# Propagation steps of a GNN kernel: nine kept blocks and a ring of four slots of two

## The reference

```python
wn = w * inv_sqrt_out[s] * inv_sqrt_in[d]
def step(h, _):
    agg = jax.ops.segment_sum(h[s] * wn[:, None], d, num_segments=n)
    return ((1.0 - ALPHA) * agg + ALPHA * feat_0, None)
h, _ = jax.lax.scan(step, feat, None, length=K)     # K = 10 steps
```

## Time and profile before

| | |
|---|---|
| median of the runs | 6561.32 us |
| profiled execution, span | 5493.1 us (the page gives no other time of this execution) |
| median less this span | 1068 us, outside the profiled span |
| propagation steps | 2346.35 to 3129.57 us, 783.22 us |
| granted TensorE clock, mean of the span | 0.839 |
| PE, DVE, POOL busy | 59%, 56%, 65% of the span |

### The profile page before, as it was taken

How to read it: one execution, slowest core, us unless ns; L and a number is a source line. 1 busy time by engine, 2 the same in 40 slices (tenths; PEclk the granted TensorE clock), 3 DMA queues, 4 the chain that set the end, 5 groups by cost and what they waited for, 6 DMA issues and landing times.

```text
span 5493.1 us, 75492 instructions
## 1 busy us (share of the span) xinstructions
PE 3237.5 (59%) x17784; PEld 2130.2 (39%) x17785; DVE 3057.9 (56%) x9445; ACT 917.4 (17%) x2328; POOL 3581.1 (65%) x3701
## 2 busy tenths in 40 slices
PE   0000000077751666589999878776878688866666
PEld 0000000032220444433333366665666566754554
DVE  8999300199960222221111278876888688865554
ACT  1000000044410111100000022222222122212121
POOL 0006888888887777788881067774777377747776
PEclk9999999999985555599999889997999799875555
DMA  2000000133311111599999622231222222221112
GB/s 92 0 0 2 2 2 2 25 102 104 106 36 15 36 36 35 117 341 355 352 363 351 260 65 62 62 58 50 62 62 63 46 62 62 62 36 29 28 28 29
DMA packets 234405, 494.61 MB, mean 90 GB/s; under 512 B 98206, under 2 KB 148294, under 8 KB 233181
## 3 DMA queue, kind: packets, MB, share of 16 engines
q1 hardware_dynamic: 104170, 331.90, 16.8%
q0 software_dynamic: 104960, 116.98, 12.0%
q10 hardware_dynamic: 25200, 44.81, 2.2%
HBM read 426.56 MB, written 65.54 MB: 90 GB/s over the span
## 4 chain that ended last, share of the span: by engine, by line
POOL 50%; issue 22%; PE 17%; DVE 7%; DMA 2%; DVEq 1%; POOLq 1%; ACT 0%; SPq 0%; ACTq 0%
POOL arena L596 33%; PE ps L1245 15%; POOL rows_bin L565 8%; POOL rows_dst L565 8%; DVE arena L756 2%; DVE arena L698 1%; DMA arena<-table,arena 1%; PE ps L1384 1%; POOL stage_at L561 1%; PE ps L1346 1%; POOL stage L560 1%; DMA arena<-rows_dst 0%; ACT arena L1181 0%; DMA rows_dst<-stage,stage_at 0%; DVE ps L743 0%
## 5 line engine op out<-in xcount | busy, mean ns | idle before, releaser
L596 POOL DMA_INDIRECT arena<-table,arena x2080 | 1979.8, 952 | 1110.2 <-issue 629.4
L1245 PE MATMUL ps<-arena 128*128 128x96 f32 (+2 forms) x7552 | 1461.6, 340 | 959.8 <-DVE arena L858 550.8
L1245 PEld LDWEIGHTS ps<-arena 128*128 128x128 f32 (+2 forms) x7552 | 1020.4, 182 | 1422.9 <-issue 1227.2
L1245 PE MATMUL ps<-arena,hs 125*64 125x500 f32 (+2 forms) x3500 | 701.3, 542 | 31.1 <-DVEq L960 16.7
L565 POOL DMA_INDIRECT rows_dst<-stage,stage_at x400 | 526.1, 1315 | 116.5 <-issue 101.8
L882 DVE TENSOR_SCALAR arena<-iota_row_b,arena 128x128 f32<-128x128 bf16 x2080 | 584.7, 302 | 0.0
L565 POOL DMA_INDIRECT rows_bin<-stage,stage_at x400 | 492.5, 1231 | 116.7 <-issue 107.3
L565 POOL DMA_INDIRECT rows_src<-stage,stage_at x400 | 482.0, 1205 | 117.6 <-issue 110.3
L894 DVE TENSOR_TENSOR arena<-ps,arena 128x256 f32<-128x256 f32 x416 | 176.6, 424 | 520.3 <-DMA arena<-table,arena 506.7
L881 DVE TENSOR_SCALAR arena<-iota_row_b,arena 128x128 bf16<-128x128 bf16 x1664 | 460.9, 279 | 3.1 <-DVE arena L1022 1.1
L1245 PEld LDWEIGHTS ps<-arena,hs 125*64 125x64 f32 x3500 | 268.4, 137 | 420.5 <-issue 407.0
(11 more groups left out here) (244 smaller groups left out, 4532.0 us busy)
## 6 DMA issues: line engine op xcount, KB each, us to landing
arena<-dense SPq DMA_DIRECT2D x360, 750.0 KB, 7.0
dense<-arena ACTq DMA_DIRECT2D x175, 250.0 KB
arena<-table,arena POOLq DMA_INDIRECT x2080
arena<-rows_dst SPq DMA_DIRECT2D x208, 96.0 KB
arena<-dense SPq DMA_DIRECT2D x6, 1750.0 KB, 18.4
rows_bin<-stage,stage_at POOLq DMA_INDIRECT x400
rows_dst<-stage,stage_at POOLq DMA_INDIRECT x400
rows_src<-stage,stage_at POOLq DMA_INDIRECT x400
```

The costliest lines, as they stand in the source:

```text
L596: nc.gpsimd.indirect_dma_start(rows[:, u, k, 0:width], None, frm, bass.IndirectOffsetOnAxis(ap=p[:, c, j, c_other:c_other + 1].bitcast(I32 ...
L1245: return nc.tensor.matmul(to, lhsT, rhs, start=start, stop=stop, skip_group_check=True)
```

## The change

The numbers of blocks, slots and slot size change: nine blocks of a group are kept, the other 16 come in eight transfers (`NG`) of two blocks, 500 KB each, and these share a ring of `RS = 4` slots: transfer `g` lands in slot `g % 4`. SP waits for `slot_used` as before; as ACT primes the count with 4 instead of 6, the issue of a transfer now waits for the release of the one four before it. Semaphore `slot_in` exists once for each slot, and PE waits for a count that rises by two transfers in each group. The transposition of the even group before stands behind slot 2 (12 products into the group) instead of behind slot 1 (also 12). Kept blocks, last group, slots and buffers take 35250 words.

```diff
-NR = 7
-GB = 3
+NR = 9
+GB = 2
 NG = (HI - NR) // GB
-assert NR + NG * GB == HI
+RS = 4
+assert NR + NG * GB == HI and NG % RS == 0
...
-        slots = carve([128, NG, GB, CW])
+        slots = carve([128, RS, GB, CW])
...
-        slot_in = [sem(f"slot_in{g}") for g in range(NG)]
+        slot_in = [sem(f"slot_in{g}") for g in range(RS)]
...
                     for g in range(NG):
                         sp.wait_ge(slot_used, (s * (CG - 1) + c) * NG + (g + 1))
-                        sp.dma_start(slots[:, g], dense[bass.ds(c, 1), :, NR + g * GB:NR + (g + 1) * GB, :].rearrange(
-                            "o p b w -> (o p) b w")).then_inc(slot_in[g], 16)
+                        sp.dma_start(slots[:, g % RS], dense[bass.ds(c, 1), :, NR + g * GB:NR + (g + 1) * GB, :].rearrange(
+                            "o p b w -> (o p) b w")).then_inc(slot_in[g % RS], 16)
...
-            a.sem_inc(slot_used, NG)
+            a.sem_inc(slot_used, RS)
...
-                        a.wait_ge(slot_used, (s * (CG - 1) + i * 2) * NG + (p + 2) * NG)
+                        a.wait_ge(slot_used, (s * (CG - 1) + i * 2) * NG + ((p + 1) * NG + RS))
...
                             for g in range(NG):
-                                pe.wait_ge(slot_in[g], (s * (CG - 1) + c + 1) * 16)
+                                pe.wait_ge(slot_in[g % RS], (s * (CG - 1) + c) * (16 * NG // RS) + 16 * (g // RS + 1))
...
-                                    ins = times(p, h, b, slots[0:LO, g, j, :], CW, 1 if b < 2 * NR else b % 2,
+                                    ins = times(p, h, b, slots[0:LO, g % RS, j, :], CW, 1 if b < 2 * NR else b % 2,
                                                 b == NR, b >= HI - 2)
                                 ins.then_inc(slot_used, 1)
-                                if p == 1 and g == 1:
+                                if p == 1 and g == 2:
                                     turn(s * CG + c - 1, oT[:, 0, :], CB)
```

## The result

The changed kernel takes 6709.93 us in the median (4 runs, 6693.49 to 6724.85) against 6563.38 us (4 runs): ratio 1.0224, 95% interval 1.0197 to 1.0251. It is slower by about 147 us. The forecast was 6650 us, 88 us above the 6561.32 it started from, with a range of 6585 to 6735. That the kernel is slower is clear; whether by more than 2% is not, since the interval reaches down to 1.0197.

A forecast was written before the change was run, and what follows sets the result against it. The prediction took PE to bound the propagation stage, with the transfers early. Its terms, 88 - 0 to 3.6 + 0, gave about +88 us on 6561.32: 6650 us, range 6585 to 6735.

The forecast's parts named there:

- step 1: Streamed blocks in the propagation stage: 276 to 246 MB; PE waits only 3.6 us for them, so gain at most 3.6 us.
- step 2: PE's products: the same 25 per group, kept blocks rising from 7 to 9 at the same rate; 0.
- step 3: Loading the larger kept set before the stage: 3.07 MB more, hidden by PE's wait for DVE; 0, without that cover up to 8.
- step 4: Leaving the stage: last slot issue and the layer weights queued behind it on SP come 7.4 us later; 0.
- step 5: SP's issuing of transfers: eight issues per group at 0.33 us each, at least 0.83 us apart; 0.
- Step 6: The ring of four slots: blocks late at g7 and at g0 after even groups; 2.95 us a pair, 88 us.
- L: Time from issue to landing of a 512 kB transfer, taken as 3.9 us; each 0.1 us is 6 us of time.
- T: Time from a slot's release to its next use: 0.45, then L, then about 0.1; taken as 4.45 us.
- rival 1: The ring is deep enough: L 2.3 to 2.6, g7's loss absorbed, g0 late after even groups; +10 us, 6570; chance 0.12.
- rival 2: A short landing in the ring, as by the skill's fit: L 3.2 us; +44, 6605; chance 0.13.
- Rival 4: Streamed transfers: pieces of 4000 B move no faster each than those of 6000 B; +204, 6765; chance 0.05.
- Rival 3: PE's clock falls too: a quarter of the stage at 1.2 GHz, about +90 + 140, 6790; chance 0.06.

The follow-up runs named there:

- deep9: The changed kernel with eight slots in place of four, kept blocks of five groups loaded only and read as overlapping ranges; ratio 1.0005 against the kernel before.
- base: The kernel before, unchanged, profiled again: ratio 0.9998, stage 814 us at clock 0.97; PE busy about 13 us more than at 0.99, the price of two hundredths.
- change2: The changed kernel as it is, timed on a chip where the kernel before takes about 5490 us: ratio 1.0262, 5632.02 us.
- fine1: The changed kernel with one block (250 KB) to a transfer, 16 a group, in a ring of eight slots; ratio 1.0097 against the kernel before, +55 us.
- half: The changed kernel with each of the 480 transfers bringing one block (250 KB), which PE reads twice; ratio 1.0059 against the kernel before, +32 us.
- even1: The changed kernel with one block to a transfer, eight slots, and the kept products spread over the group; ratio 1.0047 against the kernel before, +26 us.
- size500: The kernel before, seven kept blocks, with the other 18 in nine transfers of 500 KB, each with its own slot; ratio 0.9997.
- even4: The changed kernel with its nine kept products spread over the group (the spread order); ratio 1.0188 against the kernel before, in a second timing 1.0181, 5593.68 us.

## Why the prediction was right, and where its size was off

**What bounds the kernel** was read rightly: PE in front, with the transfers early. deep9 reads less and gains nothing.

**Steps 1 to 5** hold. Fewer bytes (step 1): no gain, ratio 1.0005 in deep9. Products (step 2): its stage is base's, 812.9 against 814.4 us, with nine kept blocks. Kept set (step 3): PE enters the stage at 2342.58, after a wait of 16.15 us for DVE. Layer weights (step 4): their lateness shows as one wait of 1.5 us behind the stage in change2, followed by 13.2 us for ACT's copy of wnT, which was to cover it. SP (step 5): fine1 issues twice as often and is faster than the change.

**Step 6** had the mechanism: the ring, and its places. The mis-sized term is L, the time from issue to landing. I took 3.9 us; the median is 4.8 (3.8 to 6.3), and the transfers on the chain, those that PE really waits for, took 4.5 in the mean. The prediction's own slope, 6 us for each 0.1 us of L, gives 88 + 54 = 142 us by the median, which is what the stage grew by (925.25 - 783.22 = 142), but only 88 + 38 = 126 by the transfers on the chain. The reason I gave for going below the bound of 4.1 was that the row of 4.8 for 768 kB might hold queueing. It may have; but the queueing of the new, shorter transfers was to be added, and I left it in the upper end of the range alone. half shows its weight: about 1.1 us. That the median gives the growth to the microsecond is luck: the sum has no term for the clock, which fell from 0.99 to 0.97 over the stage, and by the price from base that alone is about 13 us, an estimate, close to the 16 between 126 and 142. On the other kind of chip, where the clock was 0.97 before and after, the stage grew by 127 us.

Three slips in the prediction's working change nothing. By its own T of 4.45 us g6 would also be late (5.0 + 4.45 = 9.45 against a start at 8.3), but the later wait before g7 covers it. By its slope rival 1 ends at an L of 3.0 us, not 2.9. And the upper end of the range was widened by 5 us, not 10.

**The Trainium skill's fit** (DMA: Bandwidth & Descriptors, "Anatomy of one DMA — SWDGE (gpsimd) path"), 2.0 us plus bytes over 436 GB/s, gives as an estimate 3.2 us for 512 kB and 2.6 us for 256 kB. At 256 kB the trace agrees for the least landing, 2.6 us in even1, and not for the median, 3.8. At 512 kB the least landing in change2 is 3.8 us and the median 4.8. As the landing of transfers issued from SP with several in flight, the L of rival 2, the measurement decides against it.

**The rivals.** Rival 1 (deep enough) and rival 2 (short landing) are refuted by the landings; half shows that rival 1's account of a short landing was right. Rival 4 (pieces of 4000 B) is refuted by size500. Rival 3 (the clock) is partly true: if only the levels of 1.2 and 2.4 GHz are granted, means of 0.97 and 0.98 are 4 to 6% of the stage at the lower one, in place of 2% at 0.99, far from the quarter that it was priced with. What it costs no run isolates; the price from base makes it about 13 us of the 142, and of the 38 us between the spread order and the change about 20 at most.

**What was to be seen** came as stated in kind: 480 issues of 500 KB, the waits in over a hundred places, DMA share 0.81 where 0.8 or less was given, stage start unmoved. In size it missed with L: the stage was given as 871 us and is 925.25, the waits of the weight loads as 70 to 130 us and are 180.4, the landing as about 4 and is 4.8.

## What to carry to other kernels

A ring is sized by turnaround, not by bytes: compare the time between a slot's release and its next use in the consumer's order with issue delay plus landing, and take the landing as it is under the new load, queue included, not at its least. Where memory is fixed, more and smaller slots (fine1) and an even spacing of the streamed work (even4) each give back a part, and together most (even1: +26 us in place of +139, on chips of one kind). And ask first whether the consumer waits for the stream at all: here 3.6 us in 783 was all that a lighter stream could win, and the deeper store was what kept it that small.

## What the runs showed of the hardware

- Two executions of one kernel on different chips differ by 1120 us (spans 5493.1 and 6613.3), 973 us of it behind the propagation steps, where POOL waits for transfers of 96 KB from `rows_dst` for 1176.2 us on the slower chip; the propagation steps differ by 31 us.
- 500 KB transfers landed in 4.8 us in the median at a DMA share of 0.81, and in 3.8 at best: a full us of queueing with a fifth of the engines' time idle, since the issues come in bursts.
- The granted clock of the propagation steps fell slightly with waits of 0.3 to 1.6 us that stand close together (0.97), and was 1.00 when the waits, with as long landings, were spread over the group.
